# Macaron block on one core: ScalarE's copies of the row maxima move behind the next group's first exponential

## The reference

```python
x = x + 0.5 * ffn(layernorm(x), W_up, W_gate, W_down)
x = x + attention(layernorm(x), Wq, bq, Wk, bk, Wv, bv)
x = x + 0.5 * ffn(layernorm(x), W_up, W_gate, W_down)

# attention: 16 query heads in 4 groups that share keys and values, head size 16
scores = einsum('bhqd,bhkd->bhqk', q, k) / sqrt(16)
scores = where(causal, -inf, scores)
out    = einsum('bhqk,bhkd->bhqd', softmax(scores), v)

# ffn: the three weights are made ternary first
hidden = silu(x @ up.T) * (x @ gate.T)
y      = hidden @ down.T
```

## Time and profile before

| | |
|---|---|
| Time, median of 3 (lowest, highest) | 615.65 us (613.38, 616.25) |
| The profiled execution: its time, its span | 613.52 us, 611.8 us |
| Attention, first to last step | 222.79 to 441.05 us |
| One chunk of it, 8 steps | 28.3 to 29.6 us, chunks 0 to 5 |
| Chunks 6 and 7 together | 43.27 us |
| Busy in attention (215 to 440 us) of 225 us | PE 208.54, ACT 189.63, DVE 185.07, POOL 120.21 |
| Granted TensorE clock | 1.00 throughout |

### The profile page before, as it was taken

The page is one execution under the profiler, slowest core; times in us unless marked ns, Lnnn a source line. Parts: engine busy times, 40 slices in busy tenths (PEclk is TensorE's granted clock), DMA queues, the critical chain, the costliest instruction groups (busy, mean ns, idle before and its releaser), DMA issues.

```text
span 611.8 us, 12440 instructions
## 1 busy us (share of the span) xinstructions
PE 566.2 (93%) x4276; PEld 344.7 (56%) x4276; DVE 484.4 (79%) x1850; ACT 413.2 (68%) x780; POOL 185.3 (30%) x231
## 2 busy tenths in 40 slices
PE   2879999999989889999899989998899999999998
PEld 2335566655656755666565656554445556666666
DVE  6797988889976789888988887888298687856654
ACT  4746656765645268898889888887866656665741
POOL 3022301101420234555555454557741011101100
DMA  9601101100203250514141414230111211212112
GB/s 313 211 19 34 19 18 35 35 19 18 36 0 96 46 143 6 140 36 108 54 91 56 90 56 90 81 65 5 36 35 34 53 53 36 66 49 59 35 35 70
DMA packets 69503, 37.90 MB, mean 62 GB/s; under 512 B 33856, under 2 KB 66880, under 8 KB 69440
## 3 DMA queue, kind: packets, MB, share of 16 engines
q1 hardware_dynamic: 69440, 37.11, 23.8%
HBM read 18.22 MB, written 10.49 MB: 47 GB/s over the span
## 4 chain that ended last, share of the span: by engine, by line
PE 76%; DVE 11%; ACT 8%; issue 2%; DMA 2%; SPq 1%; DVEq 0%; ACTq 0%
PE bank L1076 31%; PE bank L1088 16%; PE bank L1175 7%; PE bank L1239 6%; PE bank L1230 5%; PE bank L1202 5%; PE bank L1253 2%; PE bank L1244 2%; ACT shared L568 2%; DVE sm_out L938 2%; DVE hl L821 2%; DVE hid L806 2%; DVE stats L692 1%; PE bank L1213 1%; PE bank L1067 1%
## 5 line engine op out<-in xcount | busy, mean ns | idle before, releaser
L938 DVE CUSTOM_DVE_ANT_0 sm_out<-bank,mask 128x256 f16<-128x256 f32 (+1 forms) x512 | 153.0, 351 | 29.4 <-PE bank L1202 27.5
L464 ACT ACTIVATE silu<-bank,w_scale 128x512 f32<-128x512 f32 x128 | 87.4, 683 | 114.7 <-PE bank L1076 114.7
L806 DVE SCALAR_TENSOR_TENSOR hid<-silu,h_unit,bank 128x512 f32<-128x512 f32 x128 | 95.0, 742 | 64.5 <-ACT silu L464 64.1
L568 ACT ACTIVATE shared<-bank,qk_scale 128x512 f32<-128x512 f32 x192 | 121.3, 675 | 22.6 <-PE bank L1230 22.0
L1088 PE MATMUL bank<-wT_down,hh 128*128 128x256 f16 x512 | 118.3, 273 | 7.4 <-DVE hl L821 6.0
L1088 PE MATMUL bank<-wT_down,hl 128*128 128x256 f16 x512 | 118.2, 273 | 0.0
L821 DVE TENSOR_TENSOR hl<-hid,hh 128x512 f16<-128x512 f32 x128 | 103.2, 806 | 0.0
L1076 PE MATMUL bank<-xh,wT_up 128*128 128x512 f16 x256 | 98.0, 383 | 4.9 <-issue 2.5
L396 POOL TENSOR_TENSOR xnl<-xn,xnh 128x1024 f16<-128x1024 f32 x14 | 30.1, 2152 | 236.0 <-ACT xn L495 223.5
L1076 PE MATMUL bank<-xl,wT_up 128*128 128x512 f16 x256 | 98.0, 383 | 0.0
L1076 PE MATMUL bank<-xh,wT_gate 128*128 128x512 f16 x256 | 97.3, 380 | 0.8 <-DVE hid L806 0.7
(11 more groups left out here) (111 smaller groups left out, 751.5 us busy)
## 6 DMA issues: line engine op xcount, KB each, us to landing
q_st<-q_scratch SPq DMA_DIRECT2D x32, 256.0 KB
q_scratch<-q_hl SPq DMA_DIRECT2D x8, 512.0 KB, 3.1
out_dram<-x SPq DMA_DIRECT2D x7, 512.0 KB, 2.9
x<-in_x_dram SPq DMA_DIRECT2D x1, 3072.0 KB, 15.5
k_scratch<-k_hl SPq DMA_DIRECT2D x16, 128.0 KB, 2.4
k_st<-k_scratch SPq DMA_DIRECT2D x16, 128.0 KB
x<-in_x_dram SPq DMA_DIRECT2D x2, 512.0 KB, 4.3
shared<-in_w_up_t_dram SPq DMA_DIRECT2D x2, 512.0 KB, 6.6
```

The costliest lines, as they stand in the source:

```text
L464: act.activation(silu[:, e % 2, :], U[e % 2][:, :], ACT.Silu, scale=w_scale[:, 0:1]).then_inc(silu_ready, 1)
L568: act.activation(prob[:, place % 2, i, :], ST[(3 * place + i) % 2][:, :], ACT.Exp, scale=qk_scale[:, 4:5]).then_inc(exp_done, 1)
L806: dve.scalar_tensor_tensor(out=hid[:, e % 4, :], in0=silu[:, e % 2, :], scalar=h_unit[:, 0:1], in1=GT[e % 2][:, :], op0=ALU.mult, op1=ALU. ...
L938: ins = dve.tensor_tensor_reduce(sm_out[:, i, cols], SM[i][:, cols], mask[:, S - size:S], 1.0, MASKED, ALU.add, ALU.max, rowmax[:, seq_par ...
```

## The change

ScalarE makes its two copies of the maxima in the groups g = 1 and g = 3, behind E0 and ahead of E1, where before they stood in the groups g = 0 and g = 2 between the wait for `PV` and the copy of `PV`. The normalised tiles move from the end of their step to the same place behind E0, and the first of them from step (0,3) to step (0,2). GpSimd's `max_rest` moves to the groups 1 and 3 and there ahead of `causal`. TensorE's `outputs` of groups 1 and 3 waits for the copies, as they still have to read bank 5.

```diff
@@ GpSimd, attention_pair @@
                         if odd and g in (2, 3):
                             add_output(b - 1, g - 2, 3 - g)
+                        if g in (1, 3) and not end:
+                            max_rest(b + 1, g // 2)
                         if not (end and g == 3):
                             causal(4 * b + g + 1, (g + 1) % 2)
-                        if g in (0, 2) and not end:
-                            max_rest(b + 1, g // 2)
@@ ScalarE, attention_pair @@
                         if not (end and g == 3):
                             exps(*ahead, range(0, 1))
+                        if g in (1, 3) and not end:
+                            max_copy(b + 1, g // 2)
                         if not last:
+                            if (odd, g) in NORM_PLACES:
+                                normed_tile(NC + c + 3, 2 * c + 8, NORM_PLACES.index((odd, g)))
                             if not odd and g == 2:
                                 key_high(c + 2)
...
                         act.wait_ge(pv_ready, n + 1)
-                        if g in (0, 2) and not end:
-                            max_copy(b + 1, g // 2)
                         act.activation(oT[:, odd, g, :], PV[:, 0:S], ACT.Copy).then_inc(oT_ready, 1)
...
-                        if not last and (odd, g) in NORM_PLACES:
-                            normed_tile(NC + c + 3, 2 * c + 8, NORM_PLACES.index((odd, g)))
-
-            NORM_PLACES = [(0, 3), (1, 0), (1, 2), (1, 3)]
+
+            NORM_PLACES = [(0, 2), (1, 0), (1, 2), (1, 3)]
@@ TensorE, attention_pair @@
                         if g in (0, 2) and not end:
                             max_transposes(b + 1, k + 1, g // 2)
+                        if g in (1, 3) and not end:
+                            pe.wait_ge(mx_ready, 2 * (b + 1) + g // 2 + 1)
                         outputs(n, k, g)
```

## The result

The changed kernel takes 617.02 us, the median of 15 runs (616.2 to 619.33). The kernel before, in the same session, takes 615.46 (15 runs, 613.38 to 616.25). The ratio is 1.0043, with a 95% interval of 1.0029 to 1.0057. That is slower by some 2.6 us, where I forecast 0.8 us less. It lies within the half per cent and within my range, but on the wrong side, by more than the uncertainty.

The account below looks back on a forecast made before the run. TensorE was taken to set the pace of attention, with only its gaps to win. Chunks 0 to 5 (-0.6), chunks 6 and 7 (-0.45) and the queue (+0.25) gave -0.8 us: 614.8 us, range 611.6 to 618.0.

Parts of the forecast that it names:

- S2 0.76 us earlier: Step (1,3), six chunks: E0 no longer behind the copies, so S2 starts 0.79 us earlier.
- the wait of `outputs` for the second copy: Step (1,3): `outputs` waits for the second copy of the maxima, losing some of the 0.79 us gained at S2.
- the rest given back at the transposes: Step (1,3): output transposes still wait for the copy of `PV`, so only 0.04 us of the gain remains.
- (0,1) at -0.14: Step (0,1), six chunks: copies behind E0 leave the second `xT_copy` and E0 in time, 0.13 us gained each.
- S1 of (1,2) held by E2: After step (1,1): E2 stands behind the copies and `query_high`, so the next step's S1 is 0.14 us late.
- the lateness and the 0.46 us: Even chunks: S1's 0.14 us delay and the 0.46 us S2 wait in (1,1), both swallowed at the (1,2) transposes.
- the 0.04 us of (1,3): Step (1,3): net gain of 0.04 us left at the output transposes, kept in even chunks.
- the queue: SyncE: `load_max` and reads behind it issued 1.5 us later, charged 0.25 us once in chunk 6, between 0 and 1.3.
- This is covered: Chunks before chunk 6: the later SyncE loads cost nothing, since those queries are needed five steps later.
- the sign that I had named: Forecast is wrong if S0 waits for `mx_loaded` in more than one place of chunks 6 and 7.
- The gains in chunks 6 and 7: 0.04 us in some five steps, 0.2 us, plus 0.25 us in the last such step: 0.45 us together.
- E1 and E2 come too late: Rival, chance 0.12: copies and tiles ahead of E1 and E2 delay S0 and S1; 4.3 us lost, 619.9 us.

Follow-up runs that it names:

- e4: A with the fourth normalised tile back at the end of step (1,3), as in B; 616.56 us, ratio 1.0028 to B.
- e2: A with VectorE's second four Newton steps in step (1,2) in place of (1,1); 616.15 us, ratio 1.0023 to B.
- e1: A with GpSimd's rest of the maxima (L341) behind the causal mask of its step again; 655.23 us, ratio 1.0649 to B.
- e8: B with VectorE's second four Newton steps in step (1,2) in place of (1,1); 614.09 us, ratio 1.0003 to B.
- e6: B with only the normalised tiles moved, the maxima left in place; 612.88 us, ratio 0.9980 to B.
- B: The kernel before the change; 615.46 us in the main session.
- A: The changed kernel, with the whole change; 617.02 us, ratio 1.0043 to B.
- e5: A with the four normalised tiles back at their old places, so only the maxima move; 618.82 us, ratio 1.0082 to B.
- e14: A with e4's edit, e9's edit, and the last Newton step with the shift in (1,2); 614.18 us, ratio 0.9990 to B.
- e9: A with GpSimd's rest of the maxima ahead of the addition to x in (1,3); 616.71 us, ratio 1.0037 to B.

## Why the prediction was wrong

**Right.** The starts on ScalarE and TensorE in the odd chunks: S2 0.76 us earlier (0.79), the wait of `outputs` for the second copy, the rest given back at the transposes; (0,1) at -0.14 where I had -0.13; S1 of (1,2) held by E2 and 0.14 us later behind S0 than before (0.57 against 0.43), as computed; the added wait in `outputs`. e4 confirms that the transposes waited for the tile ahead of the copy of `PV`.

**The step that failed** is this: "In the even ones the transposes of (1,2) wait for VectorE, which this change does not touch. There the lateness and the 0.46 us are both swallowed, and the 0.04 us of (1,3) stay." VectorE's program was not touched, its time was. The change put GpSimd's L341 and the mask beside L724 and the shift, and they stood still for 0.48 and 0.42 us. The +0.98 at (1,2) comes three times, 2.9 us, of which the other places of these chunks take 0.8 back. e2 and e1 take the +0.98 away by moving either side of the pair, e8 shows that e2's edit is worth 0.76 us less where the neighbours are missing, and e6 makes the part that belongs to the shift in the kernel before. In e6 the steps (1,1) and (1,2) of an even chunk take 0.41 us more than in B, and its shift is 0.41 longer. That the cause is the operands' path into VectorE rests on rows: the instructions end together each time, and L938, with one operand in PSUM and one in SBUF, is never stretched. It started 152 times in the kernel before and 140 in A (128 x 256) while a GpSimd instruction ran, and took 0.41 to 0.43 us, as it does alone. No run changed the operands of the small steps, so that part is argued. The Trainium skill, "SBUF — State Buffer", section "Who interferes with whom", has the rule: an instruction of VectorE with two SBUF inputs and a GpSimd instruction that reads SBUF exclude each other, and whichever starts first holds the port to its end. This trace agrees, with 0.64 us in place of 0.16. The rule belonged among my rivals.

**The term that was mis-sized** is the queue: 0.25 us charged, 1.31 measured, at the end of my own bounds (0 to 1.3). Both issues moved as forecast. But I took the load at (0,0) of chunk 6 to land 2.7 us after its issue, from the end of the traffic. In A its traffic goes on until 408.0, 3.6 us after the issue, and S0 follows at 3.95. The end of the traffic is not yet the end of the wait. In e6 and e8, whose SyncE program is that of B, S0 waits for this load and starts 1.1 and 1.2 us after the traffic ends (402.75 and 405.5). In the kernel before it started 1.2 us after, 3.88 behind the issue, so there was no slack. With 3.9 us from issue to S0 in place of my 2.7 and the issue 1.24 later, the charge would have been 1.2. Over the runs this distance varies from 3.28 us (e2) to 4.26 (e8) where S0 waits for the load, and why it does is left open. And I looked at this load alone. The first half of the reads ends with a DMA issued at 400.93, whose reader starts at 404.78, 3.85 us later. In the kernel before the issue was at 396.59 and the reader at 401.27, 4.68 us later: 0.83 us of slack, where 1.5 were spent. That is the 0.68 us at (0,2), and it could have been counted. "This is covered" for chunks 0 to 5 held in A, but by a hair: e2, e4, e5 and e14 met these waits there too. And the sign that I had named came up: S0 waits for the maxima in two places of chunks 6 and 7, 0.48 us at 408.37 and 0.23 at 432.38. e9 won 0.4 us by issuing earlier, so the issue is a part of the 1.31; no run removed the whole.

**The gains in chunks 6 and 7** (0.45 us forecast, none measured) were mostly given back a few steps on: -0.24 at (0,2) of chunk 7 returned at (1,0), and a +0.13 at (0,0) of chunk 7 stays unexplained.

**The rivals.** "E1 and E2 come too late" gave the right sign for the wrong reason: S1 of (1,2) is 0.14 us late in odd chunks, which their other steps give back (0.01 us in all), and nothing else of it came. The range held the measured time, but by luck: its upper half was set up for the queue and for ScalarE's prices, not for VectorE. My odds of 0.12 for a slower kernel left out a mechanism that was in the trace: L728 of the kernel before shows 0.41 us at 297.76, beside L333, and 0.16 at 300.53, for equal work.

## What to carry to other kernels

An engine whose instructions a change does not touch can still be slowed by it: look at what runs beside it before and after, above all small VectorE steps on SBUF beside GpSimd. Here their duration in the trace varied from 0.15 to 0.69 us with nothing in the program. Where equal instructions show two durations, find the neighbour that ends at the same time before moving anything. For a moved issue, take the distance from issue to reader for every load that stands behind it on the queue, not only for the one that looks tightest.

## What the runs showed of the hardware

- VectorE steps of 128 x 8 numbers take 0.15 to 0.17 us alone and 0.5 to 0.69 beside a GpSimd instruction that started just ahead. They end 0.01 to 0.03 us behind it. Over the attention of all twelve profiles 165 such steps lasted longer than 0.19 us, and each of them ended so. This held not only for two SBUF inputs (L724, L728, L737) but also for a `tensor_scalar` with one (L719, 0.62 us beside L341 in e6 against 0.16 in the kernel before).
- VectorE instructions with one operand in PSUM and one in SBUF keep their length beside GpSimd: L938 (128 x 256) 0.41 to 0.43 us in 292 cases of B and A.
- GpSimd's L341 handles 8 partitions and holds VectorE's 128-partition step as long as a full mask does: 0.66 against 0.64 us.
- The load of the maxima, two small DMAs from SBUF to SBUF, takes 3.3 to 4.3 us from the start of its issue to the matmul that waits for it when it stands behind the reads of `q_st` (405.72 to 409.00 in e2, 400.30 to 403.82 in e6, 404.42 to 408.37 in A, 402.46 to 406.72 in e8). With next to no traffic beside it, in e1, L341's end (384.33) to the matmul (386.82) is 2.5 us, issue and all.
